# Hyperbolic attention: where the square of the logarithm is computed

## What is computed

```python
scores_euclid = jnp.einsum('bhtd,bhsd->bhts', q, k) / math.sqrt(D)
inner = -jnp.einsum('bhti,bhsi->bhts', q_hyp[..., :1], k_hyp[..., :1]) + jnp.einsum('bhtd,bhsd->bhts', q_hyp[..., 1:], k_hyp[..., 1:])
mdot = jnp.maximum(-inner, 1.0 + 1e-06)
dist = jnp.arccosh(mdot)
scores_hyper = -(dist * dist) / curv_k
scores = (1.0 - alpha) * scores_euclid + alpha * scores_hyper
scores = jnp.where(causal[None, None], scores, -jnp.inf)
attn = jax.nn.softmax(scores, axis=-1) * spike_mask
y = jnp.einsum('bhts,bhsd->bhtd', attn, v)
```

## Time and profile before

| | us |
|---|---|
| median of 3 runs | 2611.37 |
| fastest and slowest of them | 2601.76, 2616.66 |
| the profiled execution | 2620.64 |
| its span, first to last instruction | 2618.9 |
| first attention, from the first L663 to the last | 1126.9 |
| all after it | 1387.4 |

### The profile page before, as it was taken

How to read it: one execution, slowest core, us unless ns; L and a number is a source line. 1 busy time by engine, 2 the same in 40 slices (tenths; PEclk the granted TensorE clock), 3 DMA queues, 4 the chain that set the end, 5 groups by cost and what they waited for, 6 DMA issues and landing times. The chain is left out here.

```text
span 2618.9 us, 38830 instructions
## 1 busy us (share of the span) xinstructions
PE 2207.4 (84%) x12343; PEld 1169.6 (45%) x12344; DVE 1690.7 (65%) x3493; ACT 1369.2 (52%) x2634; POOL 922.6 (35%) x766
## 2 busy tenths in 40 slices
PE   4589898989999999999468899889888279999991
PEld 2244444444444444444222223223223268888881
DVE  4577878786878778676156655666662545555556
ACT  1366566766666665766225665656656223333332
POOL 4463645554463736433411211221111123333330
PEclk9677687877778786777778988788877689999996
DMA  1210111111121201110141122424524641111116
GB/s 47 66 54 20 57 41 49 49 48 38 37 61 26 62 23 57 33 33 9 39 58 33 26 58 50 113 90 110 133 81 138 261 158 48 47 45 45 48 41 200
DMA packets 140066, 172.35 MB, mean 66 GB/s; under 512 B 23873, under 2 KB 120338, under 8 KB 137874
## 3 DMA queue, kind: packets, MB, share of 16 engines
q1 hardware_dynamic: 131426, 149.58, 20.3%
q0 software_dynamic: 7488, 20.46, 2.6%
q10 hardware_dynamic: 1008, 0.54, 0.1%
HBM read 105.47 MB, written 65.01 MB: 65 GB/s over the span
## 5 line engine op out<-in xcount | busy, mean ns | idle before, releaser
L1243 DVE TENSOR_REDUCE NM<-sP 128x1 f32<-128x512 f32 x512 | 332.6, 684 | 233.4 <-PE sP L1126 231.8
L401 POOL TENSOR_TENSOR YZ<-XL 128x1280 f32<-128x1280 f32 x128 | 297.7, 2326 | 433.2 <-DVE XL L687 400.9
L1058 ACT ACTIVATE PT<-tP 128x512 f32<-128x512 f32 x512 | 285.6, 604 | 260.4 <-PE tP L1138 258.6
L476 ACT ACTIVATE YZ<-YZ,gsc 128x512 f32<-128x512 f32 (+3 forms) x512 | 321.9, 655 | 143.9 <-DVE YZ L663 143.6
L674 DVE CUSTOM_DVE_ANT_0 YZ<-SeP,YZ 128x512 f32<-128x512 f32 (+3 forms) x512 | 244.0, 487 | 228.7 <-PE SeP L541 187.1
L460 ACT ACTIVATE XL<-mP 128x512 f32<-128x512 f32 (+1 forms) x384 | 201.2, 525 | 181.3 <-PE mP L551 180.5
L566 PE MATMUL tPa<-ident,YZ 128*128 128x128 f32 x1280 | 281.4, 346 | 0.3
L1489 ACT ACTIVATE H<-hP,B1T 128x256 f32<-128x256 f32 x312 | 131.0, 471 | 264.5 <-PE hP L1568 264.4
L468 ACT ACTIVATE PTa<-tPa 128x512 f32<-128x512 f32 (+1 forms) x384 | 202.9, 529 | 91.3 <-PE tPa L572 86.9
L540 PE MATMUL SeP<-STG 48*128 48x512 f16 (+3 forms) x512 | 185.0, 361 | 59.4 <-DVE mn L674 58.5
L663 DVE SCALAR_TENSOR_TENSOR YZ<-YZ,XL 128x1280 f32<-128x1280 f32 x128 | 210.5, 1644 | 5.5 <-POOL YZ L401 5.1
(11 more groups left out here) (301 smaller groups left out, 4112.1 us busy)
## 6 DMA issues: line engine op xcount, KB each, us to landing
STG<-planes_a_scratch SPq DMA_DIRECT2D x512, 32.0 KB, 1.9
X<-in_L_ffn_W SPq DMA_DIRECT2D x32, 512.0 KB, 4.2
weight_planes<-X SPq DMA_DIRECT2D x64, 256.0 KB, 2.5
STGb<-planes_scratch SPq DMA_DIRECT2D x96, 128.0 KB, 7.0
planes_a_scratch<-HI SPq DMA_DIRECT2D x64, 128.0 KB, 1.7
planes_a_scratch<-LO SPq DMA_DIRECT2D x64, 128.0 KB, 1.8
STG<-planes_a_scratch SPq DMA_DIRECT2D x128, 64.0 KB, 2.1
Y<-results_scratch SPq DMA_DIRECT2D x16, 512.0 KB, 8.8
```

The source lines that it names most:

```text
L401: pool.tensor_tensor(YZ[:, h % NYZ, :], XL[:, h % NXL, :], XL[:, h % NXL, :], ALU.mult).then_inc(y_ready, 1)
L476: act.activation(w, w, ACT.Square, bias=gsc[:, b % 2, 1, i, hh:hh + 1], scale=gsc[:, b % 2, 0, i, hh:hh + 1]).then_inc(hyp_ready, 1)
L1058: act.activation(PT[:, p % 4, par, kt, :], tP[x % 3][:, :], ACT.Exp).then_inc(exp_done, 1)
L1243: dve.tensor_reduce(NM[:, g % 2, col:col + 1], sP[n % 2][:, :], AX.X, ALU.max, negate=True).then_inc(max_done, 1)
```

## The change

The product of XL with itself leaves POOL's list and becomes one activation in ACT's list, the function Square over the same 1280 columns, from XL into YZ. It waits for the same two semaphores as before and raises the same one. In ACT's list it stands in slot t = 2 behind the logarithm and the exponential of that slot, and ahead of the L476 piece of that slot.

```diff
@@ gpsimd
-                        h = s - 1
-                        if t == 2 and 0 <= h < HEADS:
-                            pool.wait_ge(clamped, h + 1)
-                            if h >= NYZ:
-                                pool.wait_ge(tp_full, 3 * (h - NYZ + 1))
-                            pool.tensor_tensor(YZ[:, h % NYZ, :], XL[:, h % NXL, :], XL[:, h % NXL, :], ALU.mult).then_inc(y_ready, 1)
@@ scalar
                             act.activation(PT[:, h % NPT, at:at + w], tP[xc % 2][:, 0:w], ACT.Exp, scale=-1.0).then_inc(p_ready, 1)
+                        h = s - 1
+                        if t == 2 and 0 <= h < HEADS:
+                            act.wait_ge(clamped, h + 1)
+                            if h >= NYZ:
+                                act.wait_ge(tp_full, 3 * (h - NYZ + 1))
+                            act.activation(YZ[:, h % NYZ, :], XL[:, h % NXL, :], ACT.Square).then_inc(y_ready, 1)
                         h = s - 2
```

## The result

The changed kernel takes **2529.36 us** (median of 4 runs, 2524.86 to 2530.38) against 2610.51 us before (median of 4 runs, 2601.76 to 2616.66). The ratio is 0.968, with a 95% interval of 0.966 to 0.970: 81 us or 3.1% faster. The prediction was 2576, with a range of 2547 to 2616. The direction was right; the size was not: 35 us were forecast and 81 measured.

A forecast was written before the change was run, and what follows sets the result against it. The limit moves between heads: DVE full in some preparation heads, PE or ACT nearly full elsewhere. Preparation heads -40.5 us, ACT +4 and +1.5, sum -35, from the median 2611.37 to 2576 us; range 2547 to 2616.

The forecast's parts named there:

- The mechanism on DVE: Preparation heads: L744, L762, L681 and L779 wait for POOL's product to end; they fall 1.47, 1.99, 2.08, about 2.1 us.
- The price of the Square: ACT, first attention: 128 Squares of 1280 columns at 1.25 us, between 1.22 and 1.44; in all 160 us more.
- Steps 1 to 4: Five preparation heads of a batch: -1.5, -1.0, -1.7 and -1.6 us, sum -5.8; seven batches -40.5 us.
- Step 3: Heads 566.33 and 574.27, with the square root: z starts about 1.7 us earlier, so -1.7 us a batch.
- The cost on ACT elsewhere: Heads 613.15, 620.70, 649.82 and 656.83: +0.5 us a batch, +4 for eight; last batch without preparation +1.5.
- the sum: First attention: -40.5 us from preparation heads, +4 and +1.5 on ACT, -35 us, giving 2576; chance 44%.
- heads such as 593.60: Heads full of PE, 9.84 of 9.84 us at clock 0.50; no gain counted there.
- rival A: Full ACT opens gaps, clock falls, 2.8 us a PE-full head: 2644 or 2666; 14% with rival B's harder half.
- rival D: All PE's free time in the five preparation heads is won, 9.0 us a batch: 2548; chance 14%.
- rival B: ACT bounds six heads a batch, a Square each: 2631 at worst, 2601 at half; halves share 28% and 14%.
- C: PE bounds anyhow; only head 543.31 and the plain wait gain: 2602 or 2597; 28% with rival B's milder half.
- the sign of rival B: In the first attention, long PE waits for ACT's logarithm or exponential, absent before, would show rival B.

The follow-up runs named there:

- the dummy run: Changed kernel (Square on ACT) with POOL also multiplying a 1280 column scratch area for nobody, heads 0 to 119: 2612.71 us, 1.001 of the kernel before.

## Why the prediction was wrong

**The mechanism on DVE was right.** L744, L762, L779 and L681 stood still for POOL's product, and no longer do (medians of 0.20, 0.22, 0.22 and 0.69 us; a few are still slowed by POOL's other tasks). A product put back for nobody brings the standstill and the whole time back.

**The price of the Square was right:** 1.27 us in the median against 1.25, and 1.22 to 1.44 as bounds. ACT's busy time in the stage rose by 126 us and not by 160. The other 34 are overlap: an instruction behind another starts before that one has ended (533.92 + 0.60 is 534.52, and the next starts at 534.41). The single times add up to 824 us before and 1000 after, the busy time, which counts an overlap once, to 724 and 850.

**Steps 1 to 4, the five heads, were too large.** I had -5.8 us a batch; the table gives -2.3. Position 1 gave more than forecast (-2.45 for -1.5). In the row of each trace its clock is 0.50, before and after, so the clock is not the reason: DVE's busy time fell from 11.17 us to 8.97. L744 gives 1.5 of that, as forecast. L746, L749, L751 and L752 had met POOL's tasks behind the product and take 1.8 us less together (L749 took 0.91 and takes 0.22); L754 and L681 meet POOL's tasks now and take 1.1 more. Position 2 gave about what was forecast (-0.9 for -1.0), position 5 less (-1.05 for -1.6). Step 3 failed in its sign: positions 3 and 4 together were to become 1.7 us shorter and became 2.1 longer. Three things are in it. Position 3 runs at a lower clock than before (0.71 for 0.85). I followed ACT by adding two Squares to its times, but ACT holds PE there too (PE waits 0.59 us for the logarithm before 534.57 and 0.64 us for ACT's copy before 536.24). And behind the table loads PE comes into a gap:

```profile
530.65 1.28 ACT L503 ACT_TABLE_LOAD   x1
...
532.62 1.28 ACT L511 ACT_TABLE_LOAD   x1
533.92 0.60 ACT L454 ACTIVATE XL<-mP 128x512 f32<-128x512 f32 x1
534.41 0.59 ACT L462 ACTIVATE PTa<-tPa 128x512 f32<-128x512 f32 x1
...
538.15 1.31 ACT L468 ACTIVATE YZ<-XL 128x1280 f32<-128x1280 f32 x1
```

```profile
538.23 0.29 DVE L674 CUSTOM_DVE_ANT_0 YZ<-SeP,YZ 128x128 f32<-128x128 f32 x1 [2.73 <-PE SeP L541]
```

```profile
539.31 0.38 PE L572 MATMUL tPa<-DG,shiftc 128*128 128x512 f16 x1
541.93 1.65 PE L522 MATMUL misc<-WT,xT 128*128 128x256 f32 x3 [2.24 <-DVE VSa L715]
```

ACT is busy from 530.65 to past 541, two table loads among it. DVE waits 2.73 us for PE's scores, which stand in PE's list behind its transposes of ACT's copy and four projections; then DVE's short list is late, and PE waits 2.24 us for the values (L715). The granted clock falls at 541.10, inside this wait, and position 5 has 0.67. Whether the Square alone did this no run shows: taking it off ACT here and giving it to DVE made the batch longer. ACT had 2.46 us free in position 4 before; after the change it has 0.54 in the longer head.

**The cost on ACT elsewhere was wrong in its sign, and small.** I had +0.5 us a batch for positions 8, 9, 12 and 13. They became 1.3 shorter instead. I balanced ACT's time against the head and found it equal, which was true (ACT is busy 6.62 of 6.62 us in the head at 564.47). But I took the length of the head as given, and it had DVE's standstill in it (7.55 us before, 6.62 after).

**The step that failed in size is the one that isn't in the sum.** I wrote that heads such as 593.60 "are PE's", and left them out. They are PE's at the low clock. I saw the two levels, and priced them at 2.8 us a head in rival A, where the clock falls. The same 2.8 us were never put on the other side, except as a half sentence in rival D ("a clock that rises in these heads ... would bring the same"), and there only for the five heads of the preparation, with a ceiling of 9.0 us a batch. The measured gain per batch is 12.65 us, of which 9.25 lie in four heads that the sum had at zero. Two runs bear it out for position 10: with one standstill put back it lost the high clock again in five of six batches, and with the gap on PE filled it had the high clock in spite of the standstill. For positions 6 and 7 the table shows the clock, but no run fills a gap ahead of them alone.

**The rivals.** A did not happen: the mean clock rose. B did not, but for positions 3 and 4: in positions 6 to 10 ACT is full or nearly so and the heads are shorter. C is out: the heads that are full of PE became shorter too. D had the right side and the wrong heads. The latency of x*x, which I had in step 3 only, is out as an explanation by the dummy run.

**The product on DVE** is the slowest of all runs, 2687.15 us. In the heads of the preparation DVE's list was the full one, as the prediction said, and it is so again: 11.36 of 11.74 us in position 1. The Trainium skill, page ScalarE: Activation LUTs, section Rules for kernel authors, gives multiplications to VectorE; by that rule the change would have been turned down, and the runs do not agree: 2529.36 us with the product on ACT.

**The waits.** L540 waits for L674 less than before (138.3 us in the earlier trace rows), and ACT waits for z 69 us instead of 144:

```profile
PEld SeP L540 <- DVE mn L674: 113.6, 159, 3.7
...
ACT YZ L476 <- DVE YZ L663: 68.9, 62, 5.1
```

I had named PE's waits for the logarithm as the sign of rival B. They stay short, the longest 0.8 us.

**What stays open.** Why positions 3 and 4 fall to the low clock in some batches and not in others within one trace: their lengths at position 3 go from 8.2 to 11.9 us, and the order of the work is the same. Why a gap of one length on PE is followed by the low clock in one batch and not in the next (0.93 and 1.8 us, above). And how far the rest of the low stretch (positions 1 to 3) could be lifted: one attempt raised the clock of position 3 in its trace, and the median time of the kernel stayed as it was.

## What to carry to other kernels

An instruction of 2.3 us on POOL is not free because POOL is idle: a DVE instruction that meets it may stand until it ends, so look at the longest of a DVE line beside its median, and at what POOL does then. And where PE's clock moves between two levels, price each gap on PE by what the PE-full heads behind it cost at either level, for a gain as for a loss; here one standstill of a microsecond cost four to five.

The test for it is cheap: put useless matmuls into the gap. If the kernel gets faster with more work, the gap was costing clock, and the thing to mend is what makes PE wait. Take the median of several executions for it, and not the trace of one: here single executions of the kernel before, on one chip, lay between 2595 and 2631 us.

## What was not expected of the hardware

A kernel got 0.9% faster by five matmuls a batch whose results nobody reads (2589.65 against 2611.28 us). One standstill in 16 heads cost 37 us of 2529. Taking 0.5 us of work a head off ACT, which was full in six heads a batch, moved the time by 2 us. And the cost of a product on POOL follows its length: 0, 1.3 and 2.4 us of scratch product a head give 2529, 2571 and 2613 us.
